# Attention: the steady turns project q and k once, and four DMAs exchange the halves of the sine product

## The reference, cut to what matters

```python
qkv = x @ qkv_w + qkv_b                      # (2048, 3 * 16 * 64)
q, k, v = ...                                # 16 heads of 64
# rotation of q and k, pairs (t0, t1) of neighbouring values:
r0 = t0 * cos - t1 * sin
r1 = t1 * cos + t0 * sin
attn = softmax(q @ k.T / 8)
out = (attn @ v) @ out_w + out_b
```

## Time and profile before

| | |
|---|---|
| median of 3 runs | 1850.6 us (1848.21 to 1852.71) |
| profiled execution | span 1847.4 us |
| PE busy | 1740.1 us (94%) |
| DVE busy | 1444.6 us (78%) |
| ScalarE busy | 1407.5 us (76%) |
| GpSimd busy | 1430.4 us (77%) |
| steady turns of the attention | about 60 to 1112 us |

### The profile page before, as it was taken

One profiled execution on the slowest core, in us unless ns is written; L12 is line 12 of the kernel. 1 busy time (PEld: TensorE's weight loads), 2 busy tenths in 40 slices (PEclk: granted clock), 3 DMA queues, 4 the chain that ended last, 5 costly groups with the idle time before them and its releaser, 6 DMA issues. The chain is left out here.

```text
span 1847.4 us, 53971 instructions
## 1 busy us (share of the span) xinstructions
PE 1740.1 (94%) x22856; PEld 1101.7 (60%) x22856; DVE 1444.6 (78%) x2658; ACT 1407.5 (76%) x1737; POOL 1430.4 (77%) x851
## 2 busy tenths in 40 slices
PE   5999999999999999999999999986899999978997
PEld 2466666666666666666666666675556666653454
DVE  5888888888888888888888887535988888845785
ACT  2688888888888888888888888943998888853463
POOL 6699999999999999999999999974765566624122
PEclk9899999999999999999999999998999999989998
DMA  5101010111101010101010010050111111110000
GB/s 142 25 20 31 19 31 23 27 26 28 26 24 30 21 31 19 31 23 28 23 31 23 24 26 4 2 165 18 41 40 36 37 37 37 34 26 1 1 0 24
DMA packets 71080, 56.89 MB, mean 31 GB/s; under 512 B 29196, under 2 KB 64184, under 8 KB 70840
## 3 DMA queue, kind: packets, MB, share of 16 engines
q1 hardware_dynamic: 70840, 53.44, 11.5%
HBM read 14.54 MB, written 1.05 MB: 8 GB/s over the span
## 5 line engine op out<-in xcount | busy, mean ns | idle before, releaser
L278 POOL TENSOR_TENSOR ah_probs_lo<-ah_probs,ah_probs_hi 128x1024 f16<-128x1024 f32 x512 | 1072.8, 2132 | 78.8 <-ACT ah_probs L487 78.7
L542 DVE TENSOR_REDUCE ah_part_max<-ah_p_m 128x1 f32<-128x512 f32 x1024 | 669.2, 685 | 120.9 <-PE ah_p_m L342 111.1
L484 ACT ACTIVATE ah_probs_hi<-ah_p_s 128x1024 f16<-128x1024 f32 x512 | 531.2, 1038 | 190.0 <-PE ah_p_s L358 178.8
L487 ACT ACTIVATE ah_probs<-ah_p_s 128x1024 f32<-128x1024 f32 x512 | 532.4, 1040 | 0.0
L372 PE MATMUL ah_p_o<-ah_v_hi,ah_probs_hi 128*128 128x65 f16 x4096 | 470.5, 195 | 5.7 <-POOL ah_probs_lo L278 5.1
L374 PE MATMUL ah_p_o<-ah_v_lo,ah_probs_hi 128*128 128x64 f16 x4096 | 470.5, 193 | 0.0
L376 PE MATMUL ah_p_o<-ah_v_hi,ah_probs_lo 128*128 128x65 f16 x4096 | 470.3, 194 | 0.0
L372 PEld LDWEIGHTS ah_p_o<-ah_v_hi,ah_probs_hi 128*128 128x128 f16 x4096 | 383.0, 98 | 84.3 <-DVE a_attn L565 12.3
L374 PEld LDWEIGHTS ah_p_o<-ah_v_lo,ah_probs_hi 128*128 128x128 f16 x4096 | 378.4, 98 | 91.3
L342 PE MATMUL ah_p_m<-ah_k_hi_lo,ah_q_hi_twice 128*128 128x512 f16 x1024 | 393.9, 385 | 6.6 <-DMA ah_max_q_lo<-ah_lo 3.1
L357 PE MATMUL ah_p_s<-ah_q_hi_twice,ah_k_hi_lo 128*128 128x512 f16 x1024 | 388.6, 379 | 0.8 <-ACT ah_probs L487 0.4
(11 more groups left out here) (316 smaller groups left out, 3090.0 us busy)
## 6 DMA issues: line engine op xcount, KB each, us to landing
ba_v_skew<-ba_v_own SPq DMA_DIRECT2D x64, 129.0 KB, 2.3
ah_q_hi_twice<-ah_hi SPq DMA_DIRECT2D x128, 64.0 KB, 2.0
ah_k_hi_lo<-ah_hi SPq DMA_DIRECT2D x64, 64.0 KB, 1.9
ah_one_k_hi<-ah_hi SPq DMA_DIRECT2D x64, 64.0 KB, 2.0
ah_k_hi_lo<-ah_lo SPq DMA_DIRECT2D x64, 64.0 KB, 2.0
ah_max_q_lo<-ah_lo SPq DMA_DIRECT2D x64, 64.0 KB, 2.0
ah_w_head<-in_w_heads SPq DMA_DIRECT2D x16, 160.0 KB, 2.4
bw_rot<-in_rot SPq DMA_DIRECT2D x4, 512.0 KB, 10.3
```

The source lines that it names most:

```text
L278: pool.tensor_tensor(pl[:, p % RW, :, :], pb[:, p % RP, :, :], ph[:, p % RW, :, :], ALU.subtract).then_inc(lo_pool, 1)
L484: act.activation(ph[:, p % RW, :, :], p_s[:, p % 2, :, :], ACT.Exp, scale=HD ** -0.5)
L487: act.activation(pb[:, p % RP, :, :], p_s[:, p % 2, :, :], ACT.Exp, scale=HD ** -0.5).then_inc(exp_done, 1)
L542: dve.tensor_reduce(part[:, t, 2 * half + b:2 * half + b + 1], p_m[:, b, :], AX, ALU.max).then_inc(maxed, 1)
```

## The change

From the seventh turn on, q and k are projected once, with the straight weights, in step 0. The sine product is formed from this projection with sine tables whose sign is laid out for the source half (`rotate_sin_early`). SP then sends it with four DMAs of 32 partitions x 512 x 4 bytes into a tile `swapped`, each half to the place of the other. DVE forms the cosine product in step 1 as before, from the same projection, and in step 2 waits for the four DMAs and adds `swapped`. The first six turns keep their two projections; with the other sign of the table they subtract. Weight columns are laid out anew (straight q and k, v, turned), so that from the third head on only 192 of 320 columns are loaded and split.

```diff
-W_TURNED, W_QK, W_V = slice(2 * HD, 4 * HD), slice(0, 2 * HD), slice(4 * HD, 5 * HD)
+W_QK, W_V, W_TURNED = slice(0, 2 * HD), slice(2 * HD, 3 * HD), slice(3 * HD, 5 * HD)
+LEAD_H = -(-LEAD_G // QC)
+
+def head_cols(h):
+    return W_COLS if h < LEAD_H else W_V.stop
...
+        swapped = sc.sb("rot_swapped", [P, CH])
+        swap_in = [sc.sem(f"swap_in{b}") for b in range(2)]
+        SWAP = 4 * 16
+        HALF_HD = HD // 2
...
-                        sp.dma_start(w32[:, :], a["w_heads"][h + 1]).then_inc(w_in, 16)
+                        n = head_cols(h + 1)
+                        sp.dma_start(w32[:, 0:n], a["w_heads"][h + 1][:, 0:n]).then_inc(w_in, 16)
+                    if g >= LEAD_G:
+                        sp.wait_ge(rot_done, g + 1)
+                        for at in range(0, P, HD):
+                            for to_at, from_at in ((at, at + HALF_HD), (at + HALF_HD, at)):
+                                sp.dma_start(swapped[to_at:to_at + HALF_HD, :],
+                                             rot[from_at:from_at + HALF_HD, :]).then_inc(swap_in[g % 2], 16)
                     sp.wait_ge(hi_done, g + 1)
...
-                    pool.tensor_copy(wh[:, h % 2, :], w32[:, :]).then_inc(w_hi_done, 1)
+                    n = head_cols(h)
+                    pool.tensor_copy(wh[:, h % 2, 0:n], w32[:, 0:n]).then_inc(w_hi_done, 1)
...
-                    pool.tensor_tensor(straight, straight, turned, ALU.add).then_inc(r_done, 1)
+                    pool.tensor_tensor(straight, straight, turned, ALU.subtract).then_inc(r_done, 1)
...
                     if j == 0 and g <= LAST_G:
                         pe.wait_ge(vl_done, g)
-                        project(turned_bank(g), g, W_TURNED, turned_ready)
-                    if j == 1 and g <= LAST_G:
-                        pe.wait_ge(rot_done, g + 1)
                         project(proj_bank(g), g, W_QK, proj_ready)
...
+                def rotate_sin_early(g):
+                    h, c = divmod(g, QC)
+                    dve.wait_ge(proj_ready, g + 1)
+                    if g > LEAD_G:
+                        dve.wait_ge(swap_in[(g - 1) % 2], SWAP * ((g - 1 - LEAD_G) // 2 + 1))
+                    dve.scalar_tensor_tensor(rot[:, :], proj_bank(g), bqk[:, 0, h:h + 1], sin[:, chunk(c)], ALU.add,
+                                             ALU.mult).then_inc(rot_done, 1)
 
                 def rotate_cos(g):
                     h, c = divmod(g, QC)
                     dve.wait_ge(proj_ready, g + 1)
+                    if g >= LEAD_G:
+                        dve.wait_ge(rot_done, g + 1)
...
                 def rotate_sum(g):
                     dve.wait_ge(cos_done, g + 1)
-                    dve.wait_ge(rot_done, g + 1)
-                    dve.tensor_tensor(proj_bank(g), proj_bank(g), rot[:, :], ALU.add).then_inc(r_done, 1)
+                    if g < LEAD_G:
+                        dve.wait_ge(rot_done, g + 1)
+                        dve.tensor_tensor(proj_bank(g), proj_bank(g), rot[:, :], ALU.subtract).then_inc(r_done, 1)
+                    else:
+                        dve.wait_ge(swap_in[g % 2], SWAP * ((g - LEAD_G) // 2 + 1))
+                        dve.tensor_tensor(proj_bank(g), proj_bank(g), swapped[:, :], ALU.add).then_inc(r_done, 1)
...
                         if j == 0:
-                            rotate_sin(g)
+                            rotate_sin_early(g)
```

More of the change, by code:

```diff
@@ L238, in split_weights @@
                         pool.wait_ge(v_ready, QC * (h - 1))
-                    pool.tensor_copy(wh[:, h % 2, :], w32[:, :]).then_inc(w_hi_done, 1)
+                    n = head_cols(h)
+                    pool.tensor_copy(wh[:, h % 2, 0:n], w32[:, 0:n]).then_inc(w_hi_done, 1)
                     pool.wait_ge(w_hi_done, h + 1)
-                    pool.tensor_tensor(wl[:, h % 2, :], w32[:, :], wh[:, h % 2, :], ALU.subtract).then_inc(w_split, 1)
+                    pool.tensor_tensor(wl[:, h % 2, 0:n], w32[:, 0:n], wh[:, h % 2, 0:n],
+                                       ALU.subtract).then_inc(w_split, 1)
                 split_weights(0)
@@ L2284, in _rotation_tables @@
     cos, sin = np.cos(ang).astype(f), np.sin(ang).astype(f)
-    return np.ascontiguousarray(np.tile(cos, (4, 1))), np.ascontiguousarray(np.concatenate([-sin, sin, -sin, sin]))
+    return np.ascontiguousarray(np.tile(cos, (4, 1))), np.ascontiguousarray(np.concatenate([sin, -sin, sin, -sin]))
 def _layouts(i):
@@ L2296, in _layouts @@
     turned = np.roll(order, HD // 2)
-    a["w_heads"] = c(np.concatenate([w[:, 0][..., order], w[:, 1][..., order], w[:, 0][..., turned],
-                                     w[:, 1][..., turned], w[:, 2]], -1).transpose(1, 0, 2))
+    a["w_heads"] = c(np.concatenate([w[:, 0][..., order], w[:, 1][..., order], w[:, 2], w[:, 0][..., turned],
+                                     w[:, 1][..., turned]], -1).transpose(1, 0, 2))
     b = i["L0_attn_qkv_b"].reshape(3, HEADS, HD)
```

## The result

The changed kernel takes **1895.1 us** in the median (1889.9 to 1897.6), the kernel before, on the same chip, 1851.7 (1848.2 to 1853.0): a ratio of 1.0245, with an interval from 1.0223 to 1.0267. It is slower, as forecast, but by 43.5 us instead of 13, and so outside the range. The profiled execution spans 1891.1 us, 43.7 more than that of before.

What follows compares the result with a forecast made beforehand. PE sets the pace, with DVE's chain reaching step 3's maxima matmul level with it. The exchange delays the sum 0.06 + 0.17 = 0.23 us a turn, x 58 = 13 us; 1847.4 + 13 + 3.2 gives 1864 us, range 1838 to 1880.

Steps and rivals of the forecast that it cites:

- What sets a turn: Steady attention turns: a turn changes exactly as much as the sum's start moves against the sine product, unless PE is later.
- The gain that is lost: PE's 0.64 us a turn from removed matmuls becomes a wait ahead of the maxima matmul of step 3.
- The quiet turn: Turn without late transfers: the exchange lets DVE's sum start at 609.31 against 609.25, 0.06 us later.
- the late turns: Exchange landings delayed beside instruction packets, as often as in the spread of `hi`: 0.17 us a turn, between 0.05 and 0.4.
- The clock: PE's granted clock does not fall with the new wait, PE being idle about 1.0 of 18.4 us a turn.
- (1): Rival: the exchange is hidden, landing before DVE's sum needs it; 31 us faster, 1820 us; chance 0.04.
- 2: Rival: the smaller transfers are issued faster, 0.475 us a step; 7 to 17 us faster, 1839 us; chance 0.15.
- (3): Rival: no difference, late turns pass the exchange by or steps are slightly shorter; 3.5 us at most, 1854 us; chance 0.14.
- Rival 4: Exchange transfers with rows of 2 KB land later, 0.4 us more a turn; 37 us slower, 1887 us; chance 0.09.
- GpSimd: Splitting 192 instead of 320 weight columns every fourth turn is off the path, costed at nothing; idle time no smaller.

Runs made afterwards that it cites:

- e1: Changed kernel, but the sum adds `rot` itself without waiting for the four DMAs, which still run; halves are not exchanged: 1813.6 us.
- e4: Changed kernel with DVE's sum moved from mid step 2 to its end, behind normalisation and second reduction: 1815.7 us, ratio 0.9826 to the kernel before.
- e5: Changed kernel with DVE's sum moved to the end of step 3, directly ahead of the rounding: 1833.0 us, ratio 0.9915 to the kernel before.
- e9: Changed kernel with DVE's sum moved between the two reductions of step 3: 1824.3 us, ratio 0.9863 to the kernel before.
- e7: Changed kernel with 66 unused one-column matmuls (132 PE instructions, half a fetch block) added ahead of the loop: 1878.8 us.
- e8: Changed kernel with 128 unused one-column matmuls (256 PE instructions, a whole fetch block) added ahead of the loop: 1894.7 us.
- e12: Changed kernel with sum ending step 2, two exchange DMAs, twelve spread DMAs, ScalarE issuing six in the first six turns: 1809.6 us, ratio 0.9790 to before.

## Why the prediction was right and wrong

- **What sets a turn** was right: a turn changes by as much as the sum's start against the sine product. In the changed kernel a turn is 14.43 us plus the distance from the sine product's end to the sum, in quiet and late turns alike, to 0.01 us. The exceptions are the three turns with the lower clock, which lie 1.65 above, and the first turn, 0.55 below. The same sum gives the turn before (14.43 + 3.78 = 18.21) and that of e1.
- **The gain that is lost** was right: PE's 0.64 became a wait of 1.0 us in step 3, where and from the releaser I had named (L392 behind L597). PE does not win while DVE holds the normalisation back. With a free exchange I had put 0.53 a turn; e1 has 0.63, because the reductions and the cosine product now overlap a little as well (206.81 + 1.47 = 208.28, and the cosine product starts at 208.19).
- **The quiet turn** was 0.19 longer, not 0.06. The landing was right (2.0); the fourth issue stood 1.85 instead of 1.78 behind the first, and DVE took the landing up after 0.09 instead of 0.03. Small, but times 57 it is 7 us: a difference of two chains of nearly the same length, 3.84 and 3.78, carries the whole error of either.
- **The term that failed is the late turns**: 0.17 a turn, measured 0.43 (24.5 us over 57 turns), which is more than the 0.4 that I had put as its upper end. I had named the cause, the instruction packets, but took the size from the spread, "two such packets a turn will meet it as often". They met it more often and at a worse point. Of the 30 us that the sum lacks, about 15 stand here, 7 to 8 in the quiet turn, 5 in the clock and 3 outside the steady turns. Where the packet began relative to the first of the four issues, read from the trace turn by turn, with the way from that issue to the last landing:

```
packet begins, us    before: spread of hi      after: exchange
0.0 to 1.1           5 turns, 4.16 to 4.76     7 turns, 4.22 to 4.62
1.1 to 2.9           1 turn,  4.35            19 turns, 4.25 to 5.22
2.9 to 3.2          11 turns, 4.21 to 4.49     1 turn,  5.12
```

  Before, hardly a packet fell between 1.1 and 2.9 us, when the third and fourth transfer are under way; after, nineteen did. (Four late turns of before and one of after have no packet in these rows.) And they stay: before, the packet's place moved by about 0.34 us from turn to turn and swept through the whole turn; after, with six PE instructions fewer, it moves by 0.13 in the mean, unevenly, from 4.5 us behind the sine product's end in the eleventh turn to 0.1 in the forty-fourth. The change thus altered the disturbance that I had taken over as given. 28 late turns at 0.87, instead of 21 at 0.47.
- **The clock** was wrong: I inferred from a mean idle share of 6% that it would hold. It did at gaps of 0.6 us; in three late turns, after a gap of 1.78 to 1.95, it fell for 3.4 us, which cost 4.9 us in all, a term that the sum didn't have. After three other gaps of 1.78 to 1.86 it held. A mean over a stretch doesn't tell what a single longer gap does.
- **Rivals**: the exchange isn't hidden (1), isn't issued faster (2: steps of 0.59 to 0.63), and it makes a difference (3). Rival 4, 0.4 more for rows of 2 KB, would have given 1887, near the measured time, but for the wrong reason: the quiet landings are 2.0.
- **GpSimd**: idle more, not less, as said (715.41 us busy, against 749.36).

## What to carry to other kernels

A wait for a DMA belongs behind the work that another engine needs next, in a place where its own engine would idle anyway: moving one line of DVE's list by 1.2 us was worth four per cent here (e4). Moving it further, behind the reductions of the next step, hid the DMAs wholly and gave part of the gain back (e5, e9). When a term of the sum is a disturbance with a period of its own, ask whether the change shifts its phase or its drift: its size before is one sample. And a transfer that is hidden in a loop may still be bound by its issues ahead of the loop, where another engine's queue is free.

## What the runs showed of the hardware

- An instruction packet of PE (16 KB, 0.9 to 1.6 us each) lets 64 KB transfers beside it land after up to 3.4 us instead of 2.0, and can hold the issues themselves up: the four issues of one late turn take 3.67 instead of 2.45.
- Because of this, 132 instructions whose results nothing uses made a kernel 16 us faster (e7), and 256 made no difference (e8).
- PE's steady work in the changed kernel has six gaps of 1.78 to 1.95 us. After three of them (1.95, 1.88, 1.78) the clock went from 1.00 to 0.50 (2.4 to 1.2 GHz) for 3.4 us; after the other three (1.85, 1.78, 1.86) it stayed at 1.00. In e8 it fell after five gaps of 1.68 to 1.93 and not after one of 2.01. So the length of the gap alone does not decide; what does is open.
- On ScalarE's queue an issue between partitions takes as long as on SP's, about 0.64 us, while ScalarE does nothing else (e12: four in 2.54 us, where no issue is held up).
